# Gated slot attention: compact read weights by column tiles, sigmoids as tangents, and small scalings moved between engines

## What is computed

```python
q = short_conv(h @ Wq, cq)
k = short_conv(h @ Wk, ck)
v = short_conv(h @ Wv, cv)
w = short_conv(h @ Ww, cv)
g = jax.nn.log_sigmoid(h @ Wf1 @ Wf2)
...
gt = jnp.exp(g_t)
bw = b_t[:, :, None] * w_t
Sk = Sk * gt[:, :, None, :] + k_t[..., :, None] * bw[:, :, None, :]
Sv = Sv * gt[..., None] + bw[..., None] * v_t[:, :, None, :]
s = jnp.einsum('bhd,bhdm->bhm', q_t, Sk) * SCALE
a = jax.nn.softmax(s, axis=-1)
o_t = jnp.einsum('bhm,bhmd->bhd', a, Sv)
...
o = o * jax.lax.rsqrt(jnp.mean(o * o, axis=-1, keepdims=True) + EPS)
o = o * norm_w * jax.nn.sigmoid(gate)
o = o.reshape(o.shape[0], o.shape[1], -1)
return o @ Wo
```

## Time and profile before

| | us |
|---|---|
| median of 3 runs | 5117.4 |
| lowest, highest | 5113.7, 5121.28 |
| span of the profiled execution | 5121.6 |
| slot attention within it, 73 to 3068 us | 2995 |
| TensorE busy | 4927.6 (96%) |
| VectorE busy | 4230.1 (83%) |
| ScalarE busy | 3733.4 (73%) |
| GpSimd busy | 2307.0 (45%) |

### The profile page before, as it was taken

The page is one execution under the profiler, slowest core; times in us unless marked ns, Lnnn a source line. Parts: engine busy times, 40 slices in busy tenths (PEclk is TensorE's granted clock), DMA queues, the critical chain, the costliest instruction groups (busy, mean ns, idle before and its releaser), DMA issues. The chain is left out here.

```text
span 5121.6 us, 113480 instructions
## 1 busy us (share of the span) xinstructions
PE 4927.6 (96%) x37926; PEld 3636.5 (71%) x37926; DVE 4230.1 (83%) x10048; ACT 3733.4 (73%) x9700; POOL 2307.0 (45%) x2976
## 2 busy tenths in 40 slices
PE   7999999999999999999999997979999989989899
PEld 4777777777777777777777776868756667778666
DVE  4999999999999999999999995869722378868423
ACT  4999999999999999999999995748713444446233
POOL 2555555555556565655555553741133200011332
PEclk9999999999999999999999998989999999999999
DMA  5500000000000000000000001010012471010225
GB/s 170 173 3 8 6 3 8 7 2 8 7 3 7 7 4 6 8 6 3 8 6 3 8 1 33 17 35 2 24 73 90 135 248 61 2 47 22 87 96 164
DMA packets 178268, 204.34 MB, mean 40 GB/s; under 512 B 28683, under 2 KB 165772, under 8 KB 177040
## 3 DMA queue, kind: packets, MB, share of 16 engines
q1 hardware_dynamic: 161840, 159.07, 10.2%
q0 software_dynamic: 12960, 34.63, 1.8%
q10 hardware_dynamic: 2880, 3.10, 0.2%
HBM read 157.95 MB, written 114.16 MB: 53 GB/s over the span
## 5 line engine op out<-in xcount | busy, mean ns | idle before, releaser
L471 ACT ACTIVATE sl<-PSA 128x512 f32<-128x512 f32 x58 | 34.6, 597 | 253.6 <-PE PSA L172 249.0
L1900 POOL TENSOR_TENSOR gsa_qkb<-gsa_qkb,gsa_tmpb 128x256 f32<-128x256 f32 x64 | 47.7, 745 | 316.3 <-DVE gsa_tmpb L1555 316.3
L1863 POOL TENSOR_TENSOR gsa_qka<-gsa_qka,gsa_tmpa 128x256 f32<-128x256 f32 x64 | 47.6, 744 | 312.1 <-DVE gsa_tmpa L1422 312.1
L274 DVE TENSOR_TENSOR hidden<-sl,PSA 128x512 f32<-128x512 f32 x60 | 41.2, 686 | 173.9 <-ACT sl L471 164.8
L1857 POOL TENSOR_TENSOR gsa_qkb<-IDENT,gsa_dcolb 128x512 f32<-128x512 f32 x64 | 66.5, 1039 | 187.4 <-DVE gsa_dcolb L1379 187.4
L1895 POOL TENSOR_TENSOR gsa_qka<-IDENT,gsa_dcola 128x512 f32<-128x512 f32 x64 | 66.5, 1040 | 184.3 <-DVE gsa_dcola L1517 184.3
L1111 PE MATMUL PSA<-XT,gsa_wa 128*128 128x512 f32 x256 | 123.2, 604 | 9.8 <-DMA gsa_wa<-in_w_heads 7.9
L415 DVE COPY ffn0b_hT<-PSA 128x256 f32<-128x256 f32 x71 | 30.2, 425 | 122.8 <-PE PSA L213 121.1
L415 DVE COPY ffn1b_hT<-PSA 128x256 f32<-128x256 f32 x71 | 30.1, 425 | 121.3 <-PE PSA L213 119.6
L548 POOL DMA_INDIRECT results<-ffn1b_Y,ffn1b_XI x71 | 69.8, 983 | 119.6 <-ACT ffn1b_Y L494 115.6
L548 POOL DMA_INDIRECT results<-ffn0b_Y,ffn0b_XI x71 | 69.5, 979 | 118.6 <-ACT ffn0b_Y L494 113.0
(11 more groups left out here) (853 smaller groups left out, 19369.6 us busy)
## 6 DMA issues: line engine op xcount, KB each, us to landing
pairs<-in_blank SPq DMA_DIRECT2D x2, 35904.0 KB, 128.9
ffn0b_XS<-pairs SPq DMA_DIRECT2D x71, 132.0 KB
ffn1b_XS<-pairs SPq DMA_DIRECT2D x71, 132.0 KB
gsa_wa<-in_w_heads SPq DMA_DIRECT2D x64, 128.0 KB, 2.1
X<-in_x SPq DMA_DIRECT2D x8, 512.0 KB, 8.0
mlstm_CX<-in_ctx SPq DMA_DIRECT2D x32, 128.0 KB, 2.1
ffn0b_WGU<-results SPq DMA_DIRECT2D x8, 512.0 KB, 5.2
ffn0b_WD<-results SPq DMA_DIRECT2D x8, 512.0 KB, 6.0
```

## The change

The maths is the same, written otherwise:

- **Read weights.** Of a 128 by 128 block of weights (two sequences of 64), only the two diagonal 64 by 64 squares matter. The change computes only these, with the second sequence on partitions 64 to 127: `QK[:, 512:768]`. TensorE writes 36 small matmuls in one piece, with 64 columns of weights each, to partitions 0 to 63 or 64 to 127 (`part`, `step_rights`); the diagonal comes as a seventh product, so VectorE's product with a sum and GpSimd's spreading go. VectorE joins the seven results in one piece, one product with a mask and six copies under a mask (`WMASKS`, `square_rights`), of half the elements each. The read becomes eight matmuls with a contraction of 64, into two banks, and stands behind the two slot products.
- **Sigmoids** become tangents: sigmoid(x) = 0.5 tanh(0.5 x) + 0.5. For the decay gate that is a `Tanh` and a further `Copy` with scale and bias on ScalarE; for the output gate the halves go into the bias, into `WO` (with the norm weight, by GpSimd once per head) and into an "add 1" on VectorE.
- **Small scalings**: the maximum is negated by the reduction and SCALE goes into the key-query copies (`csa`, by GpSimd); the products with 1e-5 and the addition of 1e-6 move from VectorE to GpSimd. `w` before its decays gets columns of its own (`GWV[:, 1024:1536]`), so the first decays no longer wait for its transposes.
- One more constant, `WMASKS`, is loaded at the start.

For half a, TensorE (half b has the same with other banks):

```diff
-                            last = nc.tensor.matmul(tile(PS[2][:, 0:256], e), tile(Pa[:, 2, :], e), tile(AMa[:, 2, :], e), start=True, stop=True)
-                        last.then_inc(weights_a_by_pe, 1)
-                        if within:
-                            pe.wait_ge(sigmoid_a_by_act, n * 2 + 1)
-                        for e in range(2):
-                            last = nc.tensor.matmul(tile(PS[3][:, 0:256], e), tile(Pa[:, 4, :], e), tile(AMa[:, 4, :], e), start=True, stop=True)
-                        last.then_inc(weights_a_by_pe, 1)
...
                     if within:
                         if before:
                             pe.wait_ge(sigmoid_b_by_act, m * 2 + 2)
...
                     if before:
-                        pe.wait_ge(weights_a_by_dve, m * 6 + 6)
+                        pe.wait_ge(reach_a_by_dve, m * 6 + 6)
                         for j in range(4):
-                            last = nc.tensor.matmul(tile(PS[2], j), tile(GWVa[:, 1024:1536], j), tile(QKa[:, 512:1024], j), start=True, stop=True)
-                        last.then_inc(read_a_by_pe, 1)
+                            for r in range(2):
+                                nc.tensor.matmul(PS[0][64 * r:64 * r + 64, j * 64:j * 64 + 64], part(GWVa[:, 1024:1536], 2 * j + r), part(flat(AAa), 2 * j + r), start=True, stop=True)
+                        for j in range(4):
+                            for r in range(2):
+                                nc.tensor.matmul(PS[2][64 * r:64 * r + 64, j * 32:j * 32 + 32], part(GWVa[:, 1024:1536], 2 * j + r), step_rights(AMa[:, 0, :], j, r), start=True, stop=True)
+                        for k, bank, at0 in ((1, 0, 256), (2, 2, 128), (3, 0, 384), (4, 2, 256), (5, 2, 384)):
+                            for e in range(2):
+                                for r in range(2):
+                                    last = nc.tensor.matmul(PS[bank][64 * r:64 * r + 64, at0 + e * 64:at0 + e * 64 + 64], part(Pa[:, k - 1, :], 2 * e + r), part(AMa[:, k, :], 2 * e + r), start=True, stop=True)
+                        last.then_inc(weights_a_by_pe, 1)
...
+                    if before:
+                        pe.wait_ge(weights_a_by_dve, m * 7 + 7)
+                        if within:
+                            pe.wait_ge(sigmoid_a_by_act, n * 2 + 1)
+                        for j in range(4):
+                            for r in range(2):
+                                last = nc.tensor.matmul(PS[2 + r][:, j * 64:j * 64 + 64], tile(GWVa[:, 1536:2048], j)[64 * r:64 * r + 64, :], part(QKa[64 * r:64 * r + 64, 512:768], j), start=True, stop=True)
+                        last.then_inc(read_a_by_pe, 1)
                     if within:
                         pe.wait_ge(conv_a_by_dve, n * 9 + 9)
                         pe.wait_ge(silu_a_by_act, n * 4 + 2)
```

VectorE:

```diff
-                    if before:
-                        dve.wait_ge(softmax_a_by_act, m * 2 + 1)
-                        for j in range(4):
-                            last = nc.vector.tensor_tensor_reduce(tile(WTa[:, :], j), tile(CAa[:, :], j), tile(WTa[:, :], j), 1.0, 0.0, ALU.mult, ALU.add, dcola[:, j:j + 1])
-                        last.then_inc(diagonal_a_by_dve, 1)
...
-                        dve.wait_ge(weights_a_by_pe, m * 6 + 5)
-                        dve.wait_ge(weights_a_by_dve, m * 6 + 3)
-                        dve.sem_inc(passed_by_dve, 1)
-                        nc.vector.copy_predicated(rights(QKa[:, 512:1024], 8), packs(MASKS[:, 3, :].bitcast(I32), 8), packs(PS[0][:, 0:256], 8)).then_inc(weights_a_by_dve, 1)
...
+                        dve.wait_ge(weights_a_by_pe, m + 1)
+                        nc.vector.tensor_tensor(QKa[:, 512:768], PS[0][:, 0:256], WMASKS[:, 0:256], ALU.mult).then_inc(weights_a_by_dve, 1)
+                        dve.wait_ge(weights_a_by_dve, m * 7 + 1)
+                        dve.sem_inc(passed_by_dve, 1)
+                        nc.vector.copy_predicated(square_step_rights(QKa[:, 512:768]), WMASKS[:, 256:384].bitcast(I32).rearrange("p (h u t) -> p h u t", h=2, u=2), PS[2][:, 0:128].rearrange("p (h u t) -> p h u t", h=2, u=2)).then_inc(weights_a_by_dve, 1)
+                        dve.wait_ge(weights_a_by_dve, m * 7 + 2)
+                        dve.sem_inc(passed_by_dve, 1)
+                        nc.vector.copy_predicated(square_rights(QKa[:, 512:768], 2), packs(level_mask(1), 2), packs(PS[0][:, 256:384], 2)).then_inc(weights_a_by_dve, 1)
+                        dve.wait_ge(weights_a_by_dve, m * 7 + 3)
+                        dve.sem_inc(passed_by_dve, 1)
+                        nc.vector.copy_predicated(square_rights(QKa[:, 512:768], 4), packs(level_mask(2), 4), packs(PS[2][:, 128:256], 4)).then_inc(weights_a_by_dve, 1)
...
+                        dve.sem_inc(passed_by_dve, 1)
+                        nc.vector.copy_predicated(square_rights(QKa[:, 512:768], 32), packs(level_mask(5), 32), packs(PS[2][:, 384:512], 32)).then_inc(weights_a_by_dve, 1)
...
-                        nc.vector.scalar_tensor_tensor(SGa[:, :], SGa[:, :], NW[:, 0:1], PS[2][:, :], ALU.mult, ALU.mult).then_inc(onorm_a_by_dve, 1)
+                        for r in range(2):
+                            last = nc.vector.scalar_tensor_tensor(of_part(SGa[:, :], r), of_part(SGa[:, :], r), 1.0, PS[2 + r][:, 0:256].rearrange("p (j t) -> p j t", j=4), ALU.add, ALU.mult)
+                        last.then_inc(onorm_a_by_dve, 1)
...
-                        dve.wait_ge(onorm_a_by_pool, m * 2 + 1)
-                        nc.vector.tensor_scalar(den2a[:, :], den2a[:, :], 1e-5, None, ALU.mult).then_inc(onorm_a_by_dve, 1)
...
-                        nc.vector.reduce_max(mxb[:, :], tiles(PS[7][:, :]), AX.X).then_inc(softmax_b_by_dve, 1)
+                        nc.vector.reduce_max(nmxb[:, :], tiles(PS[7][:, :]), AX.X, negate=True).then_inc(softmax_b_by_dve, 1)
```

ScalarE:

```diff
-                        act.wait_ge(softmax_a_by_dve, m * 2 + 2)
+                        act.wait_ge(softmax_a_by_dve, m + 1)
                         for j in range(4):
-                            last = nc.scalar.activation(tile(CAa[:, :], j), tile(PS[3], j), ACT.Exp, bias=nmxa[:, j:j + 1], scale=SCALE, accum_out=dena[:, j:j + 1])
+                            last = nc.scalar.activation(tile(CAa[:, :], j), tile(PS[3], j), ACT.Exp, bias=nmxa[:, j:j + 1], accum_out=dena[:, j:j + 1])
...
                         act.wait_ge(gated_a_by_pe, n * 2 + 1)
-                        nc.scalar.activation(GWVa[:, 0:512], PS[3][:, :], ACT.Sigmoid).then_inc(sigmoid_a_by_act, 1)
+                        nc.scalar.activation(GWVa[:, 0:512], PS[3][:, :], ACT.Tanh, scale=0.5).then_inc(tanh_a_by_act, 1)
+                        act.wait_ge(tanh_a_by_act, n + 1)
+                        nc.scalar.activation(GWVa[:, 0:512], GWVa[:, 0:512], ACT.Copy, scale=0.5, bias=0.5).then_inc(sigmoid_a_by_act, 1)
```

GpSimd, and the new helpers:

```diff
+        def square_rights(t, b):
+
...
+        def part(t, i):
+            return t[:, i * 64:(i + 1) * 64]
+
...
-                        pool.wait_ge(onorm_a_by_dve, m * 3 + 3)
+                        if gq == 0:
+                            pool.wait_ge(out_weights_dma, hq * 16 + 16)
+                            nc.gpsimd.tensor_tensor(WO[:, :], WO[:, :], NW[:, 0:1].to_broadcast([128, 256]), ALU.mult).then_inc(out_weights_by_pool, 1)
+                        pool.wait_ge(onorm_a_by_dve, m * 2 + 2)
                         nc.gpsimd.tensor_tensor(r4a[:, :], r0a[:, :], NEGHALF[:, :], ALU.pow).then_inc(onorm_a_by_pool, 1)
                     if within:
-                        pool.wait_ge(wnorm_a_by_dve, n * 1 + 1)
+                        pool.wait_ge(wnorm_a_by_act, n * 1 + 1)
+                        nc.gpsimd.tensor_tensor(ssa[:, :], ssa[:, :], EPSW[:, :], ALU.add).then_inc(wnorm_a_by_pool, 1)
+                        pool.wait_ge(wnorm_a_by_pool, n * 4 + 1)
```

404 lines of the change are left out of this document (190 added, 214 removed).

## The result

| | us |
|---|---|
| before, median of 4 runs | 5118.67 |
| changed kernel, median of 4 runs (lowest, highest) | 6011.92 (6003.63, 6018.1) |
| ratio, 95% interval | 1.1753 (1.1739 to 1.1768) |
| span of its profiled execution | 6001.7 |
| slot attention within it, 73 to 3948 us | 3875 |

The change makes the kernel 893 us slower; the prediction said 465 and a range that ends at 5740. The span grew by 6001.7 - 5121.6 = 880 us and the slot attention by 3875 - 2995 = 880 us: nothing happened elsewhere.

A forecast was written before the change was run, and what follows sets the result against it. VectorE was taken to set the pace before; afterwards a ring through ScalarE and TensorE: 22.46 + 5.15 - 0.92 + 0.25, 27.0 us per half against 23.31. Over 126 halves that adds 466 us: 5583 us, range 5440 to 5740.

The forecast's parts named there:

- The ring: Slot attention's cycle of waits through ScalarE and TensorE: 22.46 us per half before, 27.0 after the change.
- The clock: Warning sign: a granted clock below 1.00 in slot attention, where TensorE now pauses, would make it slower than the range.
- The sum is made on the ring: Per half in slot attention: 22.46 us plus 5.15 of additions, less 0.92, plus 0.25 for GpSimd, giving 27.0.
- 1.09 and 6.75 as before: From the read's start to ScalarE's SiLU 1.09 us, then 6.75 to the key-query product, both unchanged.
- +0.2: The read's added wait for VectorE's chain: 2.6 us plus 0.2 of signals, against 2.60 of TensorE's work.
- ScalarE's two parts: ScalarE's stretches of the ring: up to the output gate, 0.92 us shorter; from the read onward, 1.09 and 6.75.
- The small products: TensorE's 36 products for the read weights: 28 at 0.063, 8 at 0.059, plus 0.1; 2.35 us per half.
- VectorE sets the pace and TensorE has 1.2 us of slack: Slot attention before the change: VectorE's list bounds the 23.31 us half; TensorE's list is 22.1 us.
- 22.1 was to become 21.9: TensorE's work list per half of slot attention: 22.1 us before, 21.9 us with the change.
- The ring that does not close: Rival: ScalarE need not wait for the read, TensorE's list decides; 22.2 us per half, 4978 us; chance 0.09.
- The table switch of 2.66 us: Shorter-ring rival: 1.28 load plus 1.38 drain, taking 1.98 us off ScalarE; 25.6 us per half, 5407; chance 0.06.

The follow-up runs named there:

- e5: Changed kernel, same work reordered: small products split and early, read before the second projection, VectorE's chain of seven behind the second decays; 5102 us, ratio 1.0000.
- e6: As e5, but VectorE's chain of seven stays behind the q tap and the last decays, as in the changed kernel; 5616 us, ratio 1.1002.
- e9: Kernel before, with only the read moved behind the second projection and the two slot products; 5419 us, ratio 1.0629.
- e1_fill: Changed kernel with eight extra identity transposes on TensorE in each of two pauses, before the tangent-waiting projection and after the read; 5688 us, ratio 1.1121.
- e7: Kernel before with only the small scalings of the change; 5012 us, ratio 0.9827.
- e11: As e5, with GpSimd's scaling of the output weights earlier in its list; 5091 us, ratio 0.9987.
- e10: Kernel before with the small scalings and the tangents, GpSimd's scaling of the output weights placed earlier in its list; 5010 us, ratio 0.9830.
- e2: Changed kernel with the 36 small weight products moved ahead of the projection that waits for the output gate's tangent; 5635 us, ratio 1.1016.
- e3: As e2, with the read also moved ahead of the two slot products, behind the second projection; 5524 us, ratio 1.0797.

## Why the prediction was wrong

- **The ring, its course and the place of each wait: right.** L1251 waited for `gsa_sgb` (1.85 us, about 2 foretold), L1292 for the SiLU (1.73, 1.9 foretold), L1257 to L1268 took 2.25 us (2.35). ScalarE stood still ahead of L1761, for 6.24 us where some 4 were foretold. e5, e6 and e9 show that the order makes it, in both directions.
- **The clock: the step that failed.** "The sum is made on the ring" takes the way from the read to the key-query product as "1.09 and 6.75 as before", ScalarE's time, and gives TensorE's products in it, L1292 to L1325, no term of their own. That holds while they take the 4.34 us of before, since ScalarE needs 2027.29 - 2022.43 = 4.86 us from L1292's start to the end of its last SiLU; it holds only at a granted clock of 1.00, which the earlier trace rows show for an engine that is busy for 2966 of 2995 us. The list worked out in the same passage pauses three times in each half (about 2, 0.2 and 1.9 us). The fall stood under what would make the prediction wrong, without a price. What the runs showed: 7.72 instead of 4.82 us for that stretch, which then arrives 2.86 us behind ScalarE's SiLU; 6012 - 5688 = 324 us of the 429 that were missing.
- **The ring itself was 0.6 to 0.75 us too short** (27.54 in the timeline above, 27.75 in e1_fill; the other 105 us). The "+0.2" for VectorE's chain was 0.95: L1529 to L1547 end after 3.39 us, not 2.8, since each copy that waits for the one before starts 0.45 to 0.6 us after it. L1251 took 1.91 us to the next start instead of 1.72, L1268 1.82. Against it, ScalarE's two parts were 0.4 us shorter than taken.
- **The small products: right.** 20 of 64 columns in 1.29 us (L1264 to L1268) are 0.065 each, 0.063 were taken; the 8 of 32 columns (L1260) 0.055. The Trainium skill's sixty cycles whatever the width (TensorEngine Tiling (Array Packing), Instruction Overhead) is the better of the two ways to see it, since half the columns save only 0.01 us. That page's Key Properties also say that changing the tiling mode drains TensorE, a rule that speaks against this change and that I had left out. L1268 behind the block is 0.10 us longer than 1.72 and L1251 ahead of it 0.19, which would fit it, and no run here separates it.
- **"VectorE sets the pace and TensorE has 1.2 us of slack": half right.** e7 gained 0.71 us and then stood at 22.66, so the slack was 0.65. I counted matmuls in units of 0.215 to 0.222 us; the same list from start to start, with its waits of 0.07 to 0.1 us, is longer. And the compact weights leave it no shorter, as e11's 20.07 us against e10's 20.03 show, where 22.1 was to become 21.9.
- **The rivals.** The ring that does not close had no chance also for that reason: with a TensorE list as long as e10's it would have given about 5010 us at best, what e10 gives, and not 4978. The table switch of 2.66 us did not show: from the copy of the values to the end of the output gate's sigmoid took 3.28 us before and 2.65 in the changed kernel without its wait for TensorE, 0.63 less, the load's 1.30 less the copy's 0.68.

## What to carry to other kernels

Shortening every engine's list does nothing for a wait that goes round several engines: follow it from release to release, and when a change moves instructions, count what now stands between the one that waits and the one that is waited for. Where the new order lets TensorE pause once or more per stage, price the granted clock too: take the stretch behind the pauses at 0.50 and see whether it becomes the last to arrive. And time the parts of a change apart: the smallest one here, a few instructions of four columns off VectorE's list, was worth 1.7%, and lay hidden under the order of the largest.

## What the hardware showed that was not expected

- Pauses of 1.85 us and less, none of them long beside the matmuls around them, brought TensorE's granted clock to 0.50 for some 6.8 us in 16 of 19 halves, in one stretch or in two; 3.9 us of useless matmuls per half made the kernel 5.4% faster (6012 to 5688 us).
- The fall is not a fixed answer to a pause: after the same 1.73 us it came in one half of e2 and not in its neighbour, and where it came in e2 it lasted as long as in the change or half as long (28.8 and 27.1 us per half, 25.9 without it). Two orders with the same ring, e2 and e3, differ by 2% (111 us) for the share of halves in which it comes.
- A matmul with 64 columns of weights, on half of the array, took 0.065 us in a row of its kind for 64 columns of the other operand and 0.055 for 32. The read with a contraction of 64 took 1.03 us for eight (L1151 of e1_fill to its follower, 2005.54 to 2006.57), 0.13 each, longer than the four full ones before (0.89).
